# The routing before the shared experts' sums, gate biases in four strips, four banks of y, and small weights loaded earlier

## What is computed

```python
logits = xt @ router_w + router_b
scores = jax.nn.softmax(logits, axis=-1) + router_bias
g = scores.reshape(T, 4, 4)
_, gidx = jax.lax.top_k(g.max(axis=-1), 2)          # two groups of four
masked = jnp.where(keep[:, :, None], g, -jnp.inf).reshape(T, 16)
_, idx = jax.lax.top_k(masked, 2)                   # two experts a token
gate = jnp.zeros((T, 16)).at[rows, idx].add(vals)   # their scores
for e in range(16):
    h = silu(xt @ w1[e] + b1[e]) * (xt @ w2[e] + b2[e])
    y = y + gate[:, e:e+1] * (h @ w3[e] + b3[e])
z = silu(xt @ sw1 + sb1) * (xt @ sw2 + sb2) @ sw3 + sb3
return y + z
```

## Time and profile before

| engine | busy us | share of the span |
|---|---|---|
| TensorE, matmuls | 1312.4 | 86% |
| TensorE, weight loads | 651.9 | 43% |
| VectorE | 804.9 | 53% |
| ScalarE | 430.3 | 28% |
| GpSimd | 303.3 | 20% |

### The profile page before, as it was taken

The page is one execution under the profiler, slowest core; times in us unless marked ns, Lnnn a source line. Parts: engine busy times, 40 slices in busy tenths (PEclk is TensorE's granted clock), DMA queues, the critical chain, the costliest instruction groups (busy, mean ns, idle before and its releaser), DMA issues. The chain is left out here.

```text
span 1517.5 us, 18894 instructions
## 1 busy us (share of the span) xinstructions
PE 1312.4 (86%) x5849; PEld 651.9 (43%) x5850; DVE 804.9 (53%) x1776; ACT 430.3 (28%) x1179; POOL 303.3 (20%) x194
## 2 busy tenths in 40 slices
PE   5588999889689999899979999899996989899940
PEld 1122222222454555455544555455553432577730
DVE  6887788997760457125660357315573641222224
ACT  6202412110232334224422334223333000244420
POOL 2654466661000000000000000000000043322235
PEclk9689999999899999999999999999998997899975
DMA  5000000000600100010000100000006501354647
GB/s 207 1 1 0 29 1 1 1 1 1 250 1 1 28 1 1 0 22 6 0 0 0 28 0 0 0 0 0 0 0 250 245 0 57 104 168 167 168 151 239
DMA packets 44850, 80.89 MB, mean 53 GB/s; under 512 B 21378, under 2 KB 22114, under 8 KB 44275
## 3 DMA queue, kind: packets, MB, share of 16 engines
q1 hardware_dynamic: 34962, 46.55, 8.9%
q0 software_dynamic: 7424, 21.00, 5.2%
q10 hardware_dynamic: 2400, 12.59, 2.1%
HBM read 59.10 MB, written 21.01 MB: 53 GB/s over the span
## 5 line engine op out<-in xcount | busy, mean ns | idle before, releaser
L1200 POOL DMA_INDIRECT table<-ids,slot_of x32 | 30.8, 964 | 892.6 <-DVE slot_of L1411 883.1
L975 PE MATMUL big_ps<-wo_sb,ot 128*128 128x512 f32 x384 | 176.2, 594 | 7.6 <-DVE ot L1089 7.6
L966 PE MATMUL big_ps<-ht,wq_sb 128*128 128x512 f32 x384 | 171.4, 592 | 0.0
L932 ACT ACTIVATE probs<-s_ps,npeak 128x128 f32<-128x128 f32 x256 | 91.6, 362 | 270.0 <-PE p_ps L1022 233.2
L580 DVE TENSOR_TENSOR prod<-ring_ps,v_c 128x1024 f32<-128x1024 f32 x128 | 151.8, 1216 | 28.5 <-PE ring_ps L440 28.0
L244 POOL TENSOR_TENSOR prod<-q_p,k_c 128x2048 f32<-128x2048 f32 (+1 forms) x32 | 118.0, 3725 | 66.9 <-ACT q_p L302 66.9
L399 PE MATMUL out_ps<-prod,w 64*64 64x512 f32 x1024 | 130.0, 626 | 0.0
L440 PE MATMUL ring_ps<-attn,sel 32*128 32x512 f32 x512 | 100.9, 662 | 32.9 <-DVE prod L580 20.9
L966 PEld LDWEIGHTS big_ps<-ht,wq_sb 128*128 128x128 f32 x384 | 70.1, 190 | 73.9 <-issue 72.8
L975 PEld LDWEIGHTS big_ps<-wo_sb,ot 128*128 128x128 f32 x384 | 68.0, 190 | 72.9 <-issue 65.2
L1045 DVE COPY v<-big_ps 128x384 f32<-128x384 f32 x32 | 17.8, 558 | 151.9 <-PE big_ps L958 151.9
(11 more groups left out here) (200 smaller groups left out, 1810.5 us busy)
## 6 DMA issues: line engine op xcount, KB each, us to landing
wr<-in_w_routed ACTq DMA_DIRECT2D x4, 3072.0 KB, 21.4
y_rows<-y_sb SPq DMA_DIRECT2D x48, 256.0 KB, 2.0
X<-in_x SPq DMA_DIRECT2D x4, 1024.0 KB, 9.7
ht<-in_ctx_t SPq DMA_DIRECT2D x16, 256.0 KB, 4.6
out<-X SPq DMA_DIRECT2D x16, 256.0 KB
wq_sb<-in_wq SPq DMA_DIRECT2D x1, 3072.0 KB, 15.1
wo_sb<-in_wo SPq DMA_DIRECT2D x1, 3072.0 KB, 22.3
prod<-in_ctx SPq DMA_DIRECT2D x4, 512.0 KB, 10.2
```

The source lines that it names most:

```text
L932: nc.scalar.activation(probs[:, u % 3, g2, :], s_ps[u % 2][:, g2 * P:(g2 + 1) * P], ACT.Exp, bias=npeak[:, u % 3, g2:g2 + 1], accum_out=to ...
L966: last = nc.tensor.matmul(ps[:, :], wq_sb[:, c, (a * HC + k) * P:(a * HC + k + 1) * P], ht[:, c, :, 1, :], start=(c == 0), stop=(c == CH - 1))
L975: last = nc.tensor.matmul(ps[:, :], ot[:, a % 2, c, k * P:(k + 1) * P], wo_sb[:, a * HC + c, :], start=(c == 0), stop=(c == HC - 1))
```

## The change

The loads of the router weights, the rows of constants, the triangle, the biases `b3`, the token ids and the shared weights leave `route`; SP issues them at the end of its list in `top1_lora`, into tiles that are now allocated before the second attention. `route` takes six buffers for normalised rows (the four gather buffers `xg` and `h_sb`), four banks to transpose into, and four banks of `y` instead of three and a separate one for counts: every use of a bank, the logits, the counts, the gates and the table among them, has its place in one list `uses` and takes the bank of the fourth use before it. The routed weights are issued by SP behind the row stores. In TensorE's list half of `up(0)` goes ahead of the transposes of the logits, the counts follow `down(0)`, the gates `down(1)`, the table's transposes come ahead of `down(6)`. In VectorE's list all of the routing up to the slots goes ahead of `hidden(2)`; only `hidden(0)`, `hidden(1)` and `add(0)` stand between. Running sums are taken over all tiles at once, in four doublings. The gates take 32 columns a tile (17 used) so that four tiles' gates are transposed together, once for all 16 tiles, and the bias matmuls of a step take the four strips of 32 rows of `gt` and `b3_sb`. The first four gathers of `routed` are issued in `route`, and the gathers of the combination have six buffers, in the space of the shared weights.

```diff
+DEEP = 4
...
+            for dst, src in early:
+                sp.dma_start(dst[:], src).then_inc(early_in, 16)
...
-        GATES_FROM = STEPS - OCTETS
-        COUNT_AT = 3
-        rw_sb = sb("rw_sb", [P, CH, 2 * E])
-        rows_sb = sb("rows_sb", [P, ROWS])
+        BIASED_FROM = STEPS - OCTETS
+        COUNT_AFTER, GATES_AFTER, TABLE_AFTER = 0, 1, 5
...
-        xn = [xn_0[:, 0, :], xn_0[:, 1, :], h_sb[:, 0, :], h_sb[:, 1, :]]
-        gates = sb("gates", [P, T, E + 1])
-        gt = sb("gt", [E + 1, DIM])
-        scores, work, among, best1, best2, left, pos = (
-            sb(n, [P, T, E]) for n in ("scores", "work", "among3", "best1", "best2", "left", "pos"))
+        xn = [xg[:, s, :] for s in range(4)] + [h_sb[:, s, :] for s in range(2)]
+        gates = sb("gates", [P, T, 32])
+        gt = sb("gt", [P, DIM])
...
+        a_ps, b_ps, y_ps = banks("a_ps"), banks("b_ps"), banks("y_ps", 4)
+        t_ps = a_ps + b_ps
+        uses = ["lt", "logits"]
+        for k in range(STEPS):
+            uses += [(k, j) for j in range(4)]
+            uses += ["count"] * (k == COUNT_AFTER) + ["gates"] * (k == GATES_AFTER) + ["table"] * (k == TABLE_AFTER)
+        order = {use: n for n, use in enumerate(uses)}
+
+        def y_bank(use):
+
+            return y_ps[order[use] % 4]
...
-            for dst, src in ((rw_sb, rw), (rows_sb, rows), (tri, tri_in), (b3_sb, b3)):
-                sp.dma_start(dst[:], src).then_inc(w_in, 16)
-            sp.dma_start(ids[:], tok_ids).then_inc(ids_in, 16)
             sp.wait_ge(ones_ready, 1)
             sp.dma_start(table.rearrange("(i p) o -> i (p o)", p=P), tab_sb[:]).then_inc(zeroed, 16)
-            sp.dma_start(w_sb[:], w_s).then_inc(ws_in, 16)
             for n in range(T):
                 sp.wait_ge(xn_ready, n + 1)
-                sp.dma_start(xn_rows[n * P:(n + 1) * P, :], xn[n % 4]).then_inc(rows_out[n % 4], 16)
-            for k in range(4):
-                sp.wait_ge(rows_out[k], 16 * (T // 4))
+                sp.dma_start(xn_rows[n * P:(n + 1) * P, :], xn[n % len(xn)]).then_inc(rows_out[n % len(xn)], 16)
+            for part in range(4):
+                sp.dma_start(wr[:, 4 * part:4 * part + 4, :], wr_in[4 * part:4 * part + 4].rearrange("e p n -> p e n"))\
+                  .then_inc(wr_here, 16)
+            wait_rows_out(sp, range(len(xn)))
...
+            wait_rows_out(pool, range(len(xn)))
+            pool.wait_ge(tok_ready, 1)
+            for i in range(DEEP):
+                nc.gpsimd.indirect_dma_start(xg[:, i, :], None, xn_rows, bass.IndirectOffsetOnAxis(ap=tok_of[:, i:i + 1], axis=0))\
+                    .then_inc(gathered[i], 16)
...
-            for part in range(4):
-                act.dma_start(wr[:, 4 * part:4 * part + 4, :], wr_in[4 * part:4 * part + 4].rearrange("e p n -> p e n"))\
-                   .then_inc(wr_here, 16)
...
-                q = k - GATES_FROM
-                if q >= 0:
-                    act.wait_ge(gates_turned, q + 1)
-                    if q >= 1:
-                        act.wait_ge(y_done, 4 * k)
-                    nc.scalar.copy(gt[:, :], y_ps[item(k, -1) % 3][0:E + 1, :]).then_inc(gt_ready, 1)
+                if k == GATES_AFTER + 1:
+                    act.wait_ge(gates_turned, 1)
+                    act.wait_ge(logits_done, 1)
+                    nc.scalar.copy(gt[:], y_bank("gates")[:, :]).then_inc(gt_ready, 1)
...
+            def take(use):
+
+                n = order[use]
+                if n >= 4:
+                    before = uses[n - 4]
+                    if before == "lt":
+                        pe.wait_ge(lt_ready, 1)
+                    elif before == "logits":
+                        pe.wait_ge(logits_out, T // 4)
+                    elif before == "count":
+                        pe.wait_ge(count_out, 1)
+                    elif before == "gates":
+                        pe.wait_ge(gt_ready, 1)
+                    elif before == "table":
+                        pe.wait_ge(tok_ready, 1)
+                    else:
+                        pe.wait_ge(added, 4 * before[0] + before[1] + 1)
+                return y_bank(use)
+
+            def down(k):
+                q = k - BIASED_FROM
+                pe.wait_ge(h_ready, k + 1)
+                for j in range(4):
+                    last = nc.tensor.matmul(take((k, j))[:, :], h_sb[:, k % 2, j * P:(j + 1) * P], w_sb[:, k // OCTETS, W3:B1],
+                                            start=True, stop=(q < 0))
+                    if q < 0:
+                        last.then_inc(y_done, 1)
+                if q >= 0:
+                    if q == 0:
+                        pe.wait_ge(gt_ready, 1)
+                    for j in range(4):
+                        strip = slice(32 * j, 32 * j + 32)
+                        nc.tensor.matmul(y_bank((k, j))[:, :], gt[strip, q * P:(q + 1) * P], b3_sb[strip, :],
+                                         start=False, stop=True).then_inc(y_done, 1)
...
+            up(0, 0)
+            pe.wait_ge(lt_ready, 1)
+            for j in range(4):
+                last = nc.tensor.transpose(y_bank("logits")[:, j * P:(j + 1) * P], lt_sb[:, j * P:(j + 1) * P], ident[:, :])
+            last.then_inc(logits_done, 1)
+            up(0, 1)
             for k in range(STEPS):
                 if k + 1 < STEPS:
-                    up(k + 1)
-                if k == COUNT_AT:
+                    up(k + 1, 0)
+                    up(k + 1, 1)
+                if k == TABLE_AFTER + 1:
+                    pe.wait_ge(tab_in, 16)
+                    take("table")
+                    nc.tensor.transpose(tab_ps, tab_sb[:, :], ident[0:MAX_TILES, 0:MAX_TILES]).then_inc(tab_turned, 1)
+                down(k)
+                if k == COUNT_AFTER:
                     pe.wait_ge(picks_ready, 1)
+                    take("count")
                     flat = among[:].rearrange("p t e -> p (t e)")
                     nc.tensor.matmul(prefix_ps, tri[:, :], flat, start=True, stop=True).then_inc(counted, 1)
                     nc.tensor.matmul(total_ps, ones[:, :], flat, start=True, stop=True).then_inc(counted, 1)
-                q = k - GATES_FROM
-                if q == 0:
+                if k == GATES_AFTER:
                     pe.wait_ge(gates_ready, 1)
-                if q >= 0:
-                    pe.wait_ge(added, 4 * k - 2)
-                    for j in range(4):
-                        last = nc.tensor.transpose(y_ps[item(k, -1) % 3][0:E + 1, j * P:(j + 1) * P],
-                                                   gates[:, 4 * q + j, :], ident[:, :])
+                    take("gates")
+                    for q in range(4):
+                        last = nc.tensor.transpose(y_bank("gates")[:, q * P:(q + 1) * P],
+                                                   gates[:, 4 * q:4 * q + 4, :].rearrange("p j e -> p (j e)"), ident[:, :])
                     last.then_inc(gates_turned, 1)
-                pe.wait_ge(h_ready, k + 1)
-                if k == 0:
-                    pe.wait_ge(logits_out, T // 4)
-                for j in range(4):
-                    y = y_ps[item(k, j) % 3][:, :]
-                    before_it = 4 * k + j + 1 - (3 if q < 0 or j == 3 else 2)
-                    if before_it >= 1:
-                        pe.wait_ge(added, before_it)
-                    if q >= 0 and j == 0:
-                        pe.wait_ge(gt_ready, q + 1)
-                    last = nc.tensor.matmul(y, h_sb[:, k % 2, j * P:(j + 1) * P], w_sb[:, k // OCTETS, W3:B1],
-                                            start=True, stop=(q < 0))
-                    if q >= 0:
-                        last = nc.tensor.matmul(y, gt[:, j * P:(j + 1) * P], b3_sb[:, :], start=False, stop=True)
-                    last.then_inc(y_done, 1)
-            pe.wait_ge(slots_ready, 2)
-            pe.wait_ge(tab_in, 16)
-            nc.tensor.transpose(tab_ps, tab_sb[:, :], ident[0:MAX_TILES, 0:MAX_TILES]).then_inc(tab_turned, 1)
             pe.wait_ge(wr_here, 64)
...
-            own.mark(V.memset(gates[:], 1.0))
+            V.tensor_scalar_add(rstd[:, :], mv[:, :, 1], EPS).then_inc(var_ready, 1)
+            V.memset(tab_sb[:], 0.0).then_inc(ones_ready, 1)
+            own.mark(V.memset(gates[:], 0.0))
+            dve.wait_ge(std_ready, 1)
+            own.done(V.reciprocal(rstd[:, :], rstd[:, :]))
+            for k in range(T):
+                if k >= len(xn):
+                    dve.wait_ge(turned, k - len(xn) + 1)
+                    dve.wait_ge(rows_out[k % len(xn)], 16 * (k // len(xn)))
+                normalise(nc, xn[k % len(xn)], X, k, mv, rstd).then_inc(xn_ready, 1)
+            own.mark(V.memset(gates[:, :, E:E + 1], 1.0))
             own.mark(V.memset(ones[:], 1.0))
-            own.mark(V.memset(before[:, 0, :], 0.0))
-            V.memset(tab_sb[:], 0.0).then_inc(ones_ready, 1)
-            deviations(nc, dve, own, mv, rstd, var_ready, std_ready)
-            dve.wait_ge(w_in, 64)
```

(64 more changed lines are left out.)

128 lines of the change are left out of this document (64 added, 64 removed).

## The result

The changed kernel took 1469.03 us in the median of four runs (1461.87 to 1471.49), the kernel before 1513.90 beside it on the same chip (1509.34 to 1518.51): ratio 0.969, 95% interval 0.965 to 0.973. The forecast was 1470, range 1461 to 1488.

What follows compares the result with a forecast made beforehand. TensorE's order, lengthened by queued waits, 17-row biases and half clock, bounds the stage; 42.4 us there, 1.3 routed and 3 combination give 46.7 off 1519.34, 1472.6, less 2.3 to the median: 1470 us, range 1461 to 1488.

Steps and rivals of the forecast that it cites:

- logits transposed: Start of routing: logits transposed at 1165.3 instead of 1167.78 us, the router's matmuls starting 5.2 us earlier.
- TensorE's idles for adds: TensorE's sums: waits of 2.8 us before the counts and 2.4 us before the gates, 5.2 in all.
- biases, per step: `down(4)` to `down(7)`: gate biases as four matmuls in four 32-row strips, 1.3 us per step.
- one fall of the clock: TensorE's sums: one of two idle stretches brings the clock down, costing 1.9 us.
- S: Stretch from ScalarE's table load at the start of `route` to the first routed transposes; 163.0 us before, 120.65 predicted.
- routed stage: First tiles of the routed experts lose less to half clock: 1.3 us gained (0 to 2.7).
- the return of all falls: Rival 1, in the sums: stalls and half clock stay, all 15.8 us of clock loss; 1484 us, chance 0.22.
- Strips overlap: Answers rival 2, bias matmuls: strips do not overlap, 2.5 us more per step; 1480 us, chance 0.05.
- No scatter was held: Answers rival 3: VectorE holds up POOL's scatters, table lands 24 us later; 1489 us, chance 0.03.
- L: The moment at which the logits are transposed in `route`, predicted at 1165.3 us.
- The slower case: Rival 4: a late table holds TensorE before `down(6)`; 1521 us at 3.0 us per scatter, chance 0.02.
- Rival 5: Better than the bounds: the clock never falls and the normalisation is shorter; 1460 us, chance 0.08.

Runs made afterwards that it cites:

- after_again: The changed kernel unchanged, run once more as yardstick: 1469.13 us, ratio 0.972 to the kernel before.
- loads_in_route: The changed kernel with the six small loads issued at the start of `route` again: 1473.27 us, ratio 0.975 to the kernel before.
- strips_one_by_one: The changed kernel with each bias matmul directly behind its `down` matmul, strips not side by side: 1478.72 us, ratio 0.977.
- biases_first: The changed kernel with half an `up` ahead of counts and gates, and bias strips ahead of the `down` matmuls: 1460.17 us, ratio 0.966.
- table_last: The changed kernel with the table's transposes and `tok_of` moved behind the last `down`: 1476.51 us, ratio 0.977.
- old_order: The changed kernel with routing and sums interleaved as before, counts and gates later, table last: 1486.88 us, ratio 0.983.

## Why the prediction was right, and where it was not

The time, the sign and the stage were right; that the median came within 1 us of the forecast is luck, as the fourth point below shows. Step by step, from the start of `route`:

| term | predicted | measured |
|---|---|---|
| logits transposed | 23.75 | 21.1 |
| from the logits to the picks | 15 | 14.7 |
| from the logits to the first scatter | 26.1 | 25.5 |
| TensorE's idles for adds | 5.2 | 2.54 + 2.08 + 0.92 = 5.5 |
| biases, per step | 1.3 | 1.07 + 2 x 0.10 = 1.3 |
| one fall of the clock | 1.9 | 0 |
| last `down` to routed transposes | 4.0 | 3.07 |
| S | 120.65 | 115.6 |
| routed stage | -1.3 | -0.2 |
| combination, first gather to last add | -3 | -3.2 |

- **Start of the routing.** I took eight tiles at half clock; the clock rose after about three, and at full clock a tile took 0.44 us from start to start (1140.68 to 1141.56 for two), not 0.6. In `after_again` it rose after seven, and the logits came 21.6 us after the start. `loads_in_route` shows that the moved loads are worth 7.9 us there. That they cost nothing where they now are was right: the second attention, from its own table load to that of `route`, took 700.2 us (before) and 700.5 (after), and 700.5 in `loads_in_route` too, without them.
- **The LoRA block.** A cost that I had not seen: `top1_lora` took 53.6 and 53.8 us in the two traces of before, and 54.8 and 56.8 in those of the changed kernel, in which VectorE's first normalisation waits 2.71 and 2.91 us for the small `desc` load, not 1.88 and 1.94. `loads_in_route` has 55.0 there without the loads at the block's end, and `strips_one_by_one`, which has them, 53.9 with a wait of 1.92: the loads are not the cause. What is stays open.
- **The clock.** I let one idle bring it down, and gave the return of all falls 22%. None came, in two traces. The falls of before belong to the 17-row matmuls: changing their depth alone to 32 lowered the median by 7.7 us, 6.3 by the ratio of 0.996, whose interval allows 3 to 10. Falls behind an idle, the only ones in my sum, are another kind: one stands in the first trace of before (1196.98), none in the second, and none behind the three idles of the changed kernel. The long fall of the earlier trace rows began 1.0 us behind an idle of 3.00 us (1254.19), so it may belong to either kind. The prediction had not named this; it spoke of scatters and idles. The mechanism by which the forecast was carried, falls going away with the change, happened for a reason I did not have.
- **The pair that I compared.** The profiled execution of before was the slowest seen: 1519.34 us, where 44 timed runs in four sets lay at 1503.9 to 1518.6 with medians of 1511 to 1514. It held 15.8 us of clock loss in the sums; the second trace's S was 154.35, 8.7 us less. My sum, 46.7 below this execution, went on from 1472.6 with only 2.3 off to the median. A typical execution of before lies at 1511.5, 5.5 below the median that I started from, and has less to gain: of 1511.5, ratios of 0.969 and 0.972 are 47 and 43 us. Two errors, an anchor too high by 3 to 6 us and a stage S estimated 5 us too slow, cancelled.
- **The profiled pair differs by 57.5 us.** Of these, 47.4 are in S, 3.2 in the combination, and 8.0 in the window attention, which is unchanged (its end at 387.80 and 379.79 us, clock 0.94 and 0.95 over the first 390) and differs nearly as much between the two traces of the changed kernel (379.79 and 386.10). It is no effect of the change; the LoRA block gives 1.2 back.
- **Routed stage.** The first eight transposes and eight `up` records stood at half clock here too (1.94 and 3.78 us), so 0.2 came of the 1.3. In `after_again` half of it came (0.8), in `biases_first` 2.5, within the bounds that I gave (0 to 2.7).
- **Rivals.** Strips overlap (`strips_one_by_one` is 12.4 us slower). No scatter was held: the 32 went out in 40.5 us, 1.26 apart. SP issued the read of the table at L+72.3 (my sum has the issue at L+73.5 and the landing at L+76.5), and the transposes, at L+80.8, waited for nothing. The slower case was far. Rival 5's two conditions both came true, no fall and a shorter normalisation, and the profiled execution of 1461.87 us is near its 1460; the median is not, because of the anchor. The gathers of the end were 1.32 us apart, where 1.35 was to show that I am right.

The single undone parts, in S: order 17.7, strips 12.4, small loads 8.3, routed weights' issue 4.5; in sum 42.9, where S fell by 38.7 to 47.4 depending on the trace of before. The order's part is mostly the table's place (10.1). The parts overlap: with the 7 us or more that the falls with 17 rows cost (154.35 against 147.4) they come to more than the whole. The four banks of `y`, the six buffers for rows and the sums in four doublings were not undone alone, so what each is worth is not shown.

What stays open is why 17 rows bring the clock down and 32 do not, and why the unchanged window attention differs by 6 to 8 us between executions. Neither was tried further.

## What to carry to other kernels

Put the chain that ends in a long round trip (scatter, read back, gather) ahead of work that only fills an engine, even if that engine idles a few microseconds for it: here 4 us of sums bought 21.6 us of wait. Before you build a sum on one profiled execution, ask how it stands to the others; stretches at half clock that come by execution belong in the range, and a term that rests on them is not owed to the change. Make matmuls with few rows fill whole strips of 32, four at a time, and put them ahead of the main matmuls of the same banks (the last was worth 1.2 us here).

## What the hardware did that was not expected

- The granted clock fell from 2.4 to 1.2 GHz in unbroken TensorE work that alternates 128-row and 17-row matmuls (two pairs at 1.78 and 2.07 us where 1.12 is full speed), in both traces of that kernel; not with 32 or 128 rows (32 rows at the same busy time, 24.57 of 26.08 us).
- Four matmuls of 32 rows by 512 in four strips: eight records in 1.14 us, against 3.43 for eight of 128 rows and 4 x 1.05 when strips and full rows alternate. The Trainium skill, TensorE: Matmul & The Clock Gate, Measured speedup vs the span model, gives 3.07 times for four row strips of 32 by 512; here it is 3.43 / 1.07 = 3.2 by the starts of the records.
- When POOL issued four gathers at the end of a block, TensorE's first work of the next block came 9.4 us after the first of them (`table_last`; 9.0 in `old_order`), where the same gathers inside the next block let it start after 3.3. How much of this is the issuing and how much the landing was not separated.
- After an idle of 1.11 us the next transposes ran once at full clock (`biases_first`) and once at half (`strips_one_by_one`), after 3.06 us in `after_again` at full clock with the matmuls behind them at half (3.52 us for eight records).
